# A shifted-window attention block: bias rows and the second group's norm moved ahead of the first scores, one schedule for all groups, and the first roots two pieces at a time

## The reference

```
h = layernorm(x) * g1 + b1;  h = roll(h, (-4, -4));  win = 8x8 windows of h
q, k, v = split(win @ qkv_w + qkv_b), 4 heads of 16
attn = softmax(q @ k.T / 4 + relative_bias + shift_mask)
x = x + roll_back(windows_back((attn @ v) @ proj_w + proj_b))
h2 = gelu((layernorm(x) * g2 + b2) @ fc1_w + fc1_b) @ fc2_w + fc2_b
out = x + h2
```

## Time and profile before

| | before |
|---|---|
| median of three runs | 554.5 us (551.46 to 554.52) |
| the profiled execution | 554.71 us, span 552.4 us |
| busy in the span | PE 485.2 us (88%), DVE 347.2, ACT 384.4, POOL 361.0 |
| mean granted clock of PE | 0.972 |
| first scores to last scores (start on DVE) | 39.41 to 371.45 us |

### The profile page before, as it was taken

The page is one execution under the profiler, slowest core; times in us unless marked ns, Lnnn a source line. Parts: engine busy times, 40 slices in busy tenths (PEclk is TensorE's granted clock), DMA queues, the critical chain, the costliest instruction groups (busy, mean ns, idle before and its releaser), DMA issues.

```text
span 552.4 us, 18222 instructions
## 1 busy us (share of the span) xinstructions
PE 485.2 (88%) x7998; PEld 326.0 (59%) x7998; DVE 347.2 (63%) x506; ACT 384.4 (70%) x534; POOL 361.0 (65%) x380
## 2 busy tenths in 40 slices
PE   0865877889999999999999999998799999999994
PEld 0633755677677677677677777786344443444441
DVE  3718854767777777777777777873355555555521
ACT  0234765777867867867877877775588888888872
POOL 1707984957957957957957957941376677766610
PEclk9976987999999999999999999999999999999998
DMA  8213401401311311311001001000003203312323
GB/s 156 48 39 90 105 2 40 96 23 42 89 30 42 86 33 41 88 33 40 22 23 42 23 21 42 21 23 2 1 0 78 62 16 77 76 26 51 78 68 84
DMA packets 10165, 27.05 MB, mean 49 GB/s; under 512 B 3432, under 2 KB 3432, under 8 KB 8168
## 3 DMA queue, kind: packets, MB, share of 16 engines
q1 hardware_dynamic: 10088, 25.91, 20.0%
HBM read 9.11 MB, written 8.39 MB: 32 GB/s over the span
## 4 chain that ended last, share of the span: by engine, by line
PE 60%; POOL 15%; ACT 9%; DVE 9%; DMA 3%; issue 2%; SPq 1%; DVEq 0%; POOLq 0%
PE work L700 20%; PE outs L700 12%; POOL probs L378 7%; PE trans L700 7%; PE trans L798 7%; PE scores L700 5%; POOL stat_rstd L344 4%; PE work L891 3%; PE work L713 3%; POOL xn L355 3%; PE scores L838 3%; ACT probsT L640 2%; ACT vX L615 2%; DMA params<-in_params 2%; DVE probs L506 2%
## 5 line engine op out<-in xcount | busy, mean ns | idle before, releaser
L378 POOL TENSOR_TENSOR probs<-probs,negmax 128x1024 f32<-128x1024 f32 x64 | 121.7, 1901 | 61.6 <-DVE negmax L512 61.5
L506 DVE TENSOR_TENSOR probs<-scores,bias 128x1024 f32<-128x1024 f32 x64 | 78.2, 1221 | 70.3 <-PE scores L700 70.3
L344 POOL TENSOR_TENSOR stat_rstd<-stat_var,minus_half 128x8 f32<-128x8 f32 x64 | 106.0, 1656 | 5.0
L635 ACT ACTIVATE probs<-probs 128x1024 f32<-128x1024 f32 x64 | 67.7, 1058 | 40.2 <-POOL probs L378 39.4
L640 ACT ACTIVATE probsT<-trans 128x1024 f32<-128x1024 f32 x64 | 65.6, 1025 | 32.9 <-PE trans L798 32.5
L700 PE MATMUL scores<-kX,qT 32*64 32x128 f32 x2048 | 75.0, 285 | 12.3 <-DMA kX<-kT 6.1
L700 PEld LDWEIGHTS outs<-vX,probsT 128*64 128x64 f32 x2048 | 65.5, 139 | 31.0 <-issue 27.8
L349 POOL TENSOR_TENSOR xn<-x,stat_mean 128x256 f32<-128x256 f32 (+1 forms) x91 | 77.9, 873 | 5.4 <-PE work L713 1.3
L512 DVE TENSOR_REDUCE negmax<-probs 128x16 f32<-128x1024 f32 x64 | 78.1, 1220 | 2.2
L700 PE MATMUL outs<-vX,probsT 128*64 128x34 f32 x2048 | 72.7, 226 | 1.4 <-ACT probsT L640 1.4
L700 PEld LDWEIGHTS scores<-kX,qT 32*64 32x64 f32 x2048 | 58.8, 138 | 21.4 <-DMA kX<-kT 9.5
(11 more groups left out here) (73 smaller groups left out, 711.9 us busy)
## 6 DMA issues: line engine op xcount, KB each, us to landing
kX<-kT SPq DMA_DIRECT2D x128, 64.0 KB, 2.0
x<-in_x SPq DMA_DIRECT2D x32, 224.0 KB
out<-x SPq DMA_DIRECT2D x28, 224.0 KB
x<-in_x SPq DMA_DIRECT2D x32, 32.0 KB
out<-x SPq DMA_DIRECT2D x28, 32.0 KB
out<-x SPq DMA_DIRECT2D x16, 56.0 KB
params<-in_params SPq DMA_DIRECT2D x1, 709.0 KB, 11.9
out<-x SPq DMA_DIRECT2D x16, 8.0 KB
```

What stands on the lines that cost most here:

```text
L344: nc.gpsimd.tensor_tensor(stat_rstd[:, cols], stat_var[:, cols], minus_half[:, cols], ALU.pow).then_inc(ln_rstd, 1)
L378: nc.gpsimd.tensor_tensor(e, e, top, ALU.add).then_inc(shifted, 1)
L506: nc.vector.tensor_tensor(e[:, :].rearrange("q (u a m) -> q a u m", u=2, a=2), scores[:, :].rearrange("q (a u m) -> q a u m", a=2, u=2), b ...
L635: nc.scalar.activation(probs[n % 4][:, :], probs[n % 4][:, :], ACT.Exp)\
```

## The change

It edits tables and the places of four parts. `LN_STEPS_FIRST` becomes: sum, mean, centre, square and square_sum of group 1 at -1, that is ahead of the loop (`norm(-1)` on POOL and DVE, `squares_of(-1)` on ACT), its roots at 0, 0, 1, 1 and scales at 1, 1, 2, 2. `LN_STEPS_SECOND` is gone; group 2 follows `LN_STEPS`. `make_rows` is called ahead of the loop. Group 0's tasks get the same steps as the others' (without Y). QK of quarter 1 moves from -1 to step 0. The roots of group 0 are two instructions of 16 columns, not four of 8. The load of group 2 is issued at step 1 and that of group 3 at step 6 of group 0.

```diff
     if not last:
-        tasks += [(5, "XT", 0), (6, "XT", 1), (6.5, "QK", GI)] if first else \
-                 [(2, "XT", 0), (4, "XT", 1), (5, "QK", GI)]
-        tasks += [(7, "QK", GI + 1), (7.5, "V", GI)]
-    if not first:
-        tasks += [(4.5, "Y", 0), (6.5, "Y", 1)]
+        tasks += [(2, "XT", 0), (4, "XT", 1), (5, "QK", GI), (7, "QK", GI + 1), (7.5, "V", GI)]
+    tasks += [(0, "QK", 1)] if first else [(4.5, "Y", 0), (6.5, "Y", 1)]
...
-    found = [(-1, "XT", 0, 0), (-1, "XT", 0, 1), (-1, "QK", 0, 0), (-1, "V", 0, 0), (-1, "QK", 0, 1)]
+    found = [(-1, "XT", 0, 0), (-1, "XT", 0, 1), (-1, "QK", 0, 0), (-1, "V", 0, 0)]
...
+LN_STEPS_FIRST = {"sum": (-1,) * 4, "mean": (-1, None, -1, -1), "centre": (-1,) * 4,
+                  "square": (-1,) * 4, "square_sum": (-1,) * 4, "rstd": (0, 0, 1, 1),
+                  "scale": (1, 1, 2, 2)}
...
-        steps = LN_STEPS_FIRST if group == 1 else LN_STEPS_SECOND if group == 2 else LN_STEPS
+        steps = LN_STEPS_FIRST if group == 1 else LN_STEPS
...
-                if n < 0:
-                    load(2)
-                if n >= 0 and s == 2 and g + 3 < GROUPS:
+                if n in (1, STEPS - 2):
+                    load(2 if n == 1 else 3)
+                if g > 0 and s == 2 and g + 3 < GROUPS:
                     load(g + 3)
...
-            for j in range(PIECES):
-                rstd(j, j)
+            for j in (0, 2):
+                rstd(j + 1, j, 2)
...
+            norm(-1)
             for n in range(PAIRS):
                 shift_pair(n)
                 norm(n)
...
+            make_rows()
+            norm(-1)
             for n in range(PAIRS + TAIL):
...
-                if n == 0:
-                    make_rows()
...
             for kind, of, i in tasks_at(-1):
                 take(kind, of, i)
+            squares_of(-1)
```

More of the change, by code:

```diff
@@ L336, in mean, with rstd @@
                 pool.wait_ge(ln_mean, means)
-            def rstd(u, j):
-                cols = slice(j * WIN, (j + 1) * WIN)
+            def rstd(u, j, pieces=1):
+                cols = slice(j * WIN, (j + pieces) * WIN)
                 pool.wait_ge(ln_sq, u + 1)
                 nc.gpsimd.tensor_tensor(stat_var[:, cols], stat_sq[:, cols], eps[:, cols], ALU.add)\
-                  .then_inc(ln_var, 1)
+                  .then_inc(ln_var, pieces)
                 pool.wait_ge(ln_var, u + 1)
                 nc.gpsimd.tensor_tensor(stat_rstd[:, cols], stat_var[:, cols], minus_half[:, cols],
-                                        ALU.pow).then_inc(ln_rstd, 1)
+                                        ALU.pow).then_inc(ln_rstd, pieces)
             def centre(dst, src, c0, n):
@@ L526, in norm @@
             def norm(n):
-                for group, i in ln_at("square_sum", n):
-                    square_sum(PIECES * group + i, i)
+                if n >= 0:
+                    square_sums(n)
                 for group, i in ln_at("sum", n):
@@ L536, in norm, with square_sums @@
                     row_sum(x[:, group * ROW + i * PIECE:][:, 0:PIECE], i)
+                if n < 0:
+                    square_sums(n)
+            def square_sums(n):
+                for group, i in ln_at("square_sum", n):
+                    square_sum(PIECES * group + i, i)
             def sum2(s):
@@ L629, in _, with squares_of @@
             act.wait_ge(zeroed, 2)
+            def squares_of(n):
+                for group, j in ln_at("square", n):
+                    u = PIECES * group + j
+                    square(u, j, u + 1 if group == GROUPS else PIECES * group + CENTRED[j])
             for kind, of, i in tasks_at(-1):
                 take(kind, of, i)
+            squares_of(-1)
             def exp(n):
@@ L655, in _ @@
                     exp(n)
-                for group, j in ln_at("square", n):
-                    u = PIECES * group + j
-                    square(u, j, u + 1 if group == GROUPS else PIECES * group + CENTRED[j])
+                squares_of(n)
                 for kind, of, i in tasks_at(n):
```

## The result

The changed kernel takes 545.38 us (median of four runs, 544.55 to 545.89) against 553.45 (551.46 to 554.52) before: a ratio of 0.9844, 95% interval 0.9811 to 0.9877, 1.6% faster. The prediction was 544.4 us, range 539.5 to 550.5. The two profiled executions differ by more than the medians, 542.4 against 552.4 us of span: before's was at the slow end of its runs. So the trace explains 10.0 us, which is inside what the interval allows (6.8 to 10.5 us of 553.45), though above the median's 8.1.

What follows compares the result with a forecast made beforehand. PE was taken to bound the kernel from group 2 on, POOL's queue and waits the start. Group 1 starting earlier (-7.6) and running shorter (-2.7) gave -10.3: 554.7 - 10.3 = 544.4 us, range 539.5 to 550.5.

Steps and rivals of the forecast that it cites:

- the term for the clock: Group 0: 1.2 GHz until some 57 us, charged as one score block, 0.9 us, ahead of group 1.
- the sentence on the shared ports: Ahead of the first pair: `make_rows` gets cheaper where POOL idles, up to about 1 us, left out of the sum.
- The term of 1.2 us: Ahead of the loop: DVE's norm work makes pair 0 start at 40.6 instead of 39.41, +1.2 us.
- The paired roots: Group 0's norm: a root of 16 columns takes twice 1.65 us; counted at nothing.
- POOL's row: Group 0's first steps: POOL's shifts, roots and scales take 19.3 us, shift 3 ends at 62.4, 2.9 us behind before.
- the new wait for quarter 1's keys: Group 0, ahead of score 2: keys come later, but POOL's roots cover the wait with 1.5 us to spare.
- Pair 5: 66.5 forecast: Group 0: from shift 3's end to pair 5 on DVE 4.1 us, so pair 5 at 66.5, against 64.14.
- Rival B: Group 0: POOL's queue or group 2's load, landing at 65 or 66, binds more; about 550 us, chance 0.17.
- The wait for group 1's first keys: End of group 0: keys copied some 6 us ahead of their scores, so the wait of 4.64 us is gone.
- rival D: Groups 0 and 1: longer PE pauses between scores 0, 1 and 2 keep 1.2 GHz; slower, 560 us, chance 0.04.
- The term of 2.7 us: Group 1: with group 2's former contents and norm schedule it takes 41.47 us instead of 44.15, -2.7.
- Rival E: Group 0: POOL paces it in both kernels, its 5.3 us only exchanged; nothing gained, 552 to 556 us, chance 0.05.

Runs made afterwards that it cites:

- experiment 6: Changed kernel with group 0's first roots one piece at a time again: 40.35 us from pair 0 to 8, against 40.34.
- Experiments 8 to 11: Changed kernel with quarter 1's QK between scores 0 and 1 (pair 0 to 8: 39.25 us); POOL's row short (40.85); both, load early (37.60); both, load unchanged (37.60).
- experiment 3: Changed kernel with group 2's load issued early, behind the first keys: 40.19 us from pair 0 to 8, against 40.34.
- 11: Changed kernel with quarter 1's QK between scores 0 and 1 and POOL's row short, load as changed: 37.60 us from pair 0 to 8, against 40.34.
- experiment 9: Changed kernel with group 1's roots as two of 16 columns and its last scale at step 3: 40.85 us from pair 0 to 8, against 40.34.
- experiment 4: Changed kernel with dummy PE matmuls ahead of the first scores and behind quarter 1's QK: 39.96 us from pair 0 to 8, against 40.34.
- experiment 2: Changed kernel with only group 2's norm on its old table: group 1 takes 44.27 us, against 42.17.
- experiment 1: Changed kernel with group 0's old task times and group 2's old norm table back: 551.95 us, ratio 0.9966 to before.
- experiment 5: Changed kernel with `make_rows` back behind pair 0: 41.05 us from pair 0 to 8, against 40.34.
- experiment 7: Changed kernel with QK of quarter 1 back ahead of the first scores: 39.24 us from pair 0 to 8, against 40.34.

## Why the prediction was right, and where it was not

The forecast had 10.3 us for the profiled execution, the trace has 10.0, and they come from the places named: group 1's keys, and the first groups' norm. Inside, some steps were off and partly cancelled. Pair 0 to 5 was forecast at 25.9 us and took 27.93; pair 5 to 8, forecast at 14.2 with the term for the clock, took 12.41.

*Pair 0: 40.6 forecast, 39.94 measured.* `make_rows` took 1.8 us, not 3.1; the sentence on the shared ports had allowed up to about 1 less. (It read `y_upper`'s 0.93 us as beside POOL's mean; from 42.99 it ran beside shift 0, which ended at 43.86.) The eight centrings took 4.60 us, as forecast (0.58 each). DVE was ready at 38.73, and the bound was the one I had called no bound: pair 0's scores, whose keys landed for a start at 37.88. The term of 1.2 us should have been the keys' landing, not DVE's row. That the two came within 0.7 us of each other is luck.

*The paired roots: 3.3 us each forecast, 2.91 and 3.18 measured, worth nothing* (experiment 6): right.

*POOL's row: 19.3 us forecast, 19.1 measured, shift 3 to end at 62.4, measured 61.6.* The number was right, the reading was not. I said that POOL's row covers the new wait for quarter 1's keys "with 1.5 us to spare". I had followed that wait only to shift 2, where indeed it is covered. But PE's scores, behind the keys, lead through QK, the copies and V on ACT to pairs 3, 4 and 5, and there they are later than POOL's row. The failed step is thus "that new wait is covered"; 1.1 us of the 4.96 were not. Experiments 8 to 11 show the two rows: with PE's shortened, POOL's sets pair 5, 25.68 us behind pair 0 (forecast: 25.9, of which 4.1 from shift 3's end; here 61.51 to 65.60, 4.09); with POOL's shortened, or neither, PE's row sets it, 26.55 without the wait for the load (experiment 3); with both, it is 23.97. So PE's row is longer by 0.9 us at pair 5 and 1.1 at pair 8. The sum did not suffer much, and that is luck: the two rows are nearly of one length, and the 0.9 us that the forecast added behind pair 5 for a score block at the low clock is as large as the difference, though no block behind pair 5 was slow. Whether PE's row would be the shorter one without its two blocks at 1.2 GHz behind the keys was not tested.

*Pair 5: 66.5 forecast, 67.87 measured; group 1: 80.7 forecast, 80.28 measured.* The 1.4 us at pair 5 is DVE's wait for the load (67.87 against 66.49 by experiment 3's distance). Rival B was right that there is no margin, and nearly with the landing "at 65 or 66" (66.67, 8.6 us after the first issue at 58.07, not 7 to 8); DVE waiting for the load was also one of the signs named for a wrong forecast, and it came. But its price, that pair 5's delay passes on, was not: experiments 3 and 11 put it at 0.15 and 0.0 us for waits of 1.90 and 1.46, and only the 2.65 of experiment 9 showed, as 0.5. The wait for group 1's first keys went as said: back to 4.63 us when the task times go back.

*The clock: 0.9 us forecast behind pair 0, at least 0.4 measured* (experiment 4, which raised the clock for a part of the stretch only). That pauses of PE are followed by blocks at half rate was right; the granted clock was 0.50 from 34 to 54 us in the changed kernel (forecast: until 57) and 1.00 from there on, so rival D had nothing to act on. Its premise was off too: the pauses between scores 0, 1 and 2 are 1.35 and 4.96 us, and before they were 1.42 and 4.71. Before was at the low level twice more, once behind the pause of 4.64 us. Windows of the changed kernel, then one of before, with the granted clock third from the end:

```profile
34.00:54.00 20.00, 9.85 (x117) 5.45 (x114) 9.29 (x10) 6.97 (x10) 14.00 (x16) 0.50 0.10 25
54.00:80.00 26.00, 24.71 (x540) 20.10 (x544) 18.44 (x26) 21.88 (x30) 19.21 (x21) 1.00 0.37 89
```

```profile
84.60:91.40 6.80, 5.16 (x66) 3.22 (x66) 2.44 (x2) 1.51 (x3) 0.55 (x1) 0.50 0.09 22
```

*Group 1: 41.47 forecast, 42.17 measured.* The term of 2.7 us is mis-sized by 0.7. That what was gained comes from group 2's table, experiment 2 shows (2.1 us). The forecast took the whole of group 2 as it stood. The 0.7 us lie in the first four pairs: 19.51 us against 18.81, and pair 8 to 9 alone took 5.45 where pair 16 to 17 takes 4.66. The step ahead differs: it holds a Y task ahead of pair 16 and takes 5.72 us, and none ahead of pair 8, 3.62. So pair 8 comes early, and PE then waits for ACT where it doesn't behind pair 16:

```profile
83.94 0.69 PE L706 MATMUL work<-wqkv,xT 64*64 64x64 f32 x32 [0.69 <-ACT qT L610]
```

The traces show the difference; that the missing Y task is its reason is argued and not tested.

*Rival E*, POOL as the pace in both: out by the result. Its 5.3 us are the eight centrings alone (2.45 and 2.89); the three means come on top. For the first four shifts of the changed kernel it was nearer to the truth than its 0.05 said.

What stays open: how the 2.7 us that group 0 gained beside the tables (48.89 before against 46.20 in experiment 1) divides. `make_rows` holds about 0.7 of it by experiment 5, and QK's place by experiment 7 nothing that can be told (pair 8 comes 68.89 us behind the first sum with QK back, 68.72 without). The rest should be the norm of group 1 ahead of the loop, which was not moved back alone, since the task times need it. The traces show a place for it: pair 6 to 7 took 8.37 us before and 4.99 in experiment 1. Before, POOL was busy without a stop with shifts, roots and scales of group 1, ACT waited for it with exp 5, the copy for task XT stood behind that exp, and PE waited for the copy; in experiment 1 PE has no such wait.

```profile
71.96 1.06 ACT L635 ACTIVATE probs<-probs 128x1024 f32<-128x1024 f32 x1 [3.38 <-POOL probs L378]
...
73.98 0.85 PE L700 MATMUL work<-wqkv,xT 64*64 64x64 f32 x32 [2.28 <-ACT xT L602]
```

Open too is what the low clock costs behind quarter 1's keys.

## What to carry to other kernels

Follow a new wait to the end of its row, through each engine that it leads to, not to the first place where something else is later. Where two rows are of nearly one length, an experiment that shortens one shows nothing or little, and only both together show what they are worth: here nothing and 1.1 us alone, 2.7 together. When a start-up is tuned, look first at what each transfer is waited for by: here 3.9 us went from the end of the copy of quarter 1's keys to the scores (46.20 to 50.07 in the changed kernel), and 4.0 to 5.7 for quarter 0's. What fills an engine's pause ahead of such a landing cost nothing here (`make_rows`, experiment 5), until it outlasted the landing (experiment 7, 1.3 us).

## What the runs showed of the hardware

A cast on DVE from float32 to fp32r, 128 x 512, took 0.42 us with POOL idle and 2.12 us in experiment 5, where it began at 41.15 while POOL was in shift 0 (41.08 to 42.98) and ended just after it. So not only operations with two inputs are held up: this cast has one. Before, the same cast took 0.41 us, begun at 44.04, though a centring on POOL began at 44.12; that the one that begins first goes on unhindered fits these rows and was not tested. The Trainium skill (SBUF — State Buffer, "SBUF: two separate sides") names both kinds, DVE in a mode with two ports and DVE with two SBUF inputs, as holders of the shared pair; that the cast is of the first kind fits the number and was not tested further.

A root (power of -1/2) on POOL took 1.65 us for 8 columns and 2.91 for 16; by these two, about 0.39 us are fixed and 0.16 go with each column, an estimate. Beside DVE's scale and bias additions the 16 columns took 3.18.
